# A graph network on one core: sums before one-hot products in each step of the build

## The reference

```python
# layer 0: gated, weighted sum over the edges
h = sigmoid(x @ W_gate + b_gate) * (x @ W)
out = segment_sum(edge_weight[:, None] * h[dst], src, N)
# layer 1: plain sum, then a matrix
out = segment_sum(x[src], dst, N) @ W.T + b
# layer 2: messages of both ends, summed, then an update
msg = concat(x[src], x[dst]) @ W_msg + b_msg
out = concat(x, segment_sum(msg, dst, N)) @ W_upd + b_upd
# layer 3: hypergraph convolution (nodes -> hyperedges -> nodes), batch norm, relu
out = relu(gamma * (o - mean(o)) * rsqrt(var(o) + eps) + beta)
```

## Time and profile before

| what | value |
|---|---|
| median of 3 runs | 2465.7 us |
| the profiled execution | 2461.7 us, its span 2459.8 us |
| mean granted TensorE clock | 0.978 |
| TensorE busy | 2293.2 us, 93% of the span |
| VectorE, ScalarE busy | 1444.7 us and 1279.8 us |
| HBM read and written | 257.85 MB, 92.19 MB |

### The profile page before, as it was taken

How to read it: one execution, slowest core, us unless ns; L and a number is a source line. 1 busy time by engine, 2 the same in 40 slices (tenths; PEclk the granted TensorE clock), 3 DMA queues, 4 the chain that set the end, 5 groups by cost and what they waited for, 6 DMA issues and landing times.

```text
span 2459.8 us, 72172 instructions
## 1 busy us (share of the span) xinstructions
PE 2293.2 (93%) x28669; PEld 2025.0 (82%) x28669; DVE 1444.7 (59%) x3422; ACT 1279.8 (52%) x2875; POOL 57.0 (2%) x57
## 2 busy tenths in 40 slices
PE   3689999999999989999889998999998999998997
PEld 3469898998899889988768887888887888887886
DVE  8779999998899988989643233234333111222223
ACT  3689999999899989989342222222221000011112
POOL 3500000000000000000000000000000000000000
PEclk9799999999999999999989999999999999999998
DMA  7799999999999999999989999999998999999997
GB/s 188 182 213 195 201 212 207 209 210 200 189 208 208 196 203 195 205 197 205 226 202 291 290 290 290 248 261 257 258 261 214 291 290 290 264 252 241 269 268 188
DMA packets 1528563, 569.80 MB, mean 232 GB/s; under 512 B 869815, under 2 KB 1526971, under 8 KB 1528152
## 3 DMA queue, kind: packets, MB, share of 16 engines
q1 hardware_dynamic: 1524709, 559.04, 104.0%
q0 software_dynamic: 1200, 4.10, 0.6%
q10 hardware_dynamic: 2370, 2.71, 0.4%
HBM read 257.85 MB, written 92.19 MB: 142 GB/s over the span
## 4 chain that ended last, share of the span: by engine, by line
PE 63%; SPq 16%; ACT 9%; DMA 5%; issue 4%; DVE 3%; POOLq 1%; another core or an unknown queue 0%; POOL 0%; DVEq 0%; ACTq 0%
PE ps L804 35%; SPq L542 8%; SPq L489 5%; ACT stage L1348 4%; PE ps L732 4%; ACT stage L1329 3%; PE ps L733 3%; PE ps L734 3%; PE ps L701 3%; PE ps L702 3%; PE ps L703 3%; PE ps L709 3%; DMA wt<-stage 3%; SPq L486 2%; PE ps L725 1%
## 5 line engine op out<-in xcount | busy, mean ns | idle before, releaser
L1348 ACT CAST stage<-ps 128x784 f16<-128x784 f32 x784 | 657.4, 838 | 18.0 <-PE ps L734 10.5
L804 PE MATMUL ps<-Ha,a_tiles 128*128 128x258 f16 x4606 | 523.9, 273 | 7.2 <-DVE Ha L1124 7.2
L732 PE MATMUL ps<-hot_c,hot_r 128*128 128x98 f16 x3136 | 502.7, 210 | 13.5 <-DVE hot_c L1046 10.4
L804 PEld LDWEIGHTS ps<-Ha,a_tiles 128*128 128x128 f16 x4606 | 449.9, 98 | 73.5 <-DVE Ha L1124 7.6
L733 PE MATMUL ps<-hot_c,hot_r 128*128 128x98 f16 x3136 | 500.4, 210 | 0.0
L734 PE MATMUL ps<-hot_c,hot_r 128*128 128x98 f16 x3136 | 498.8, 209 | 0.0
L701 PE MATMUL ps<-g_in,wt 128*128 128x128 f16 x2401 | 426.9, 220 | 29.2 <-DMA wt<-stage 20.1
L1329 ACT CAST stage<-ps 128x392 f16<-128x392 f32 x784 | 405.1, 517 | 43.4 <-PE ps L709 40.8
L703 PE MATMUL ps<-g_in,wt 128*128 128x128 f16 x2401 | 426.9, 220 | 0.0
L702 PE MATMUL ps<-g_in,wt 128*128 128x128 f16 x2401 | 426.9, 220 | 0.0
L1046 DVE TENSOR_TENSOR hot_c<-hot_c,meta 128x1568 f16<-128x1568 f16 x392 | 379.2, 967 | 0.0
(11 more groups left out here) (199 smaller groups left out, 2338.6 us busy)
## 6 DMA issues: line engine op xcount, KB each, us to landing
a_tiles<-counts_by_source SPq DMA_DIRECT2D x147, 1600.0 KB, 13.2
counts_by_source<-stage SPq DMA_DIRECT2D x49, 1600.0 KB, 8.7
meta<-edge_groups SPq DMA_DIRECT2D x26, 128.0 KB, 2.4
wt<-stage SPq DMA_TRANSPOSE x198, 6.2
gated_parts<-G SPq DMA_DIRECT2D x7, 448.0 KB, 5.4
g_in<-gated_parts SPq DMA_DIRECT2D x98, 32.0 KB, 6.0
out_x<-X SPq DMA_DIRECT2D x12, 256.0 KB
edge_table<-tab ACTq DMA_DIRECT2D x1, 2040.0 KB, 10.6
```

What stands on the lines that cost most here:

```text
L732: mm(into(0), rows_, codes(0), start=v == 0, stop=True, skip_group_check=True)
L804: last = mm(ps[:, sum_bank(ph, j, c), 0:PARTS], a_slot(ph, c, i), moving[:, i], start=i == 0, stop=i == TILES - 1)
L1348: a.copy(stage[:, b, 0:2 * FULL].rearrange("p (k i) d -> p k i d", k=2)[:, :, 0:TILES, u * SET_COLS:(u + 1) * SET_COLS], of).then_inc(s("h ...
```

## The change

In each round of `build` on TensorE the group of sums is issued in front of the wait for the one-hot set and the two units, where it was issued behind them. Nothing else differs: the same instructions, the same groups in the same step, the same semaphores and counts. The other engines' programs are unchanged.

```diff
                     for h in range(TILE_HOTS):
-                        pe.wait_ge(s("hot_ready"), j * TILE_HOTS + (h + 1))
-                        half_windows(j, c % 2, c, 2 * h)
-                        half_windows(j, c % 2, c, 2 * h + 1)
                         if not isinstance(n, int) or n >= 0:
                             g = sum_at(c, h)
                             if g == 0:
                                 loaded(n, 0)
                                 loaded(n, 1)
                             sum_some(n, cp, g)
+                        pe.wait_ge(s("hot_ready"), j * TILE_HOTS + (h + 1))
+                        half_windows(j, c % 2, c, 2 * h)
+                        half_windows(j, c % 2, c, 2 * h + 1)
```

## The result

The changed kernel takes 2533.48 us (median, 4 runs, 2529.95 to 2539.24) against 2465.8 us for the kernel before: 1.0274 times as long, 95% interval 1.0252 to 1.0296. The profiled execution took 2534.69 us with a span of 2532.8 us, 73.0 us more than before.

What follows compares the result with a forecast made beforehand. TensorE was busy in 93% of the span, with VectorE, ScalarE and DMA also close to full in the build. 52 + 18 - 2 = +68 us on the profiled 2461.7, plus 4.0 for the median, gave 2533 us; range 2500 to 2560.

Steps and rivals of the forecast that it cites:

- (a): In odd steps of the build, TensorE's wait for transposed tiles loses cover: 2.5 us longer per pair of steps.
- (g): The DMA chain up to the transposes may shorten as DMA engines get some air: 0.1 us a pair, -2 us.
- (b): SP's DMA chain starts earlier, 0.2 us for even tiles, under 0.1 for odd: 2.5 us a pair becomes 2.4.
- (f): TensorE's clock in the build drops after 14 of the 21 new stalls, 1.3 us each: 18 us.
- (e): The loop's two back edges, before steps 25 and 37: +1 us each, bounds 0 and 2.5.
- (c): ScalarE's copy of the even step's last turned block ends 0.8 us behind its last unit; the new stall hides it.
- (d): Each group of sums in the build needs a later addition by VectorE: cost 0, bounded at 221 us.
- A: Rival: in the build the wait moves as said, but the clock holds: +50 us, 2516 us; 20%.
- B: Rival: every new stall in the build drops the clock, in part for longer: 2553 to 2573 us; 10%.
- C: Rival: time from odd tile's last unit to its use shrinks to 24.2 us, clock unaffected: +35, 2501 us; 7%.
- D: Rival: faster, with odd tiles' transposes in by the even step's last unit and SP starting earlier: 2456 us; 4%.
- E: Rival: the order of groups in the build is immaterial, as ScalarE makes up for every stall: 2466 us; 4%.

Runs made afterwards that it cites:

- e1: Against the kernel before, sums put first in even steps only, odd steps in the old order: 2467.73 us, ratio 1.0024.
- e2: Against the kernel before, sums put first in odd steps only, even steps in the old order: 2516.42 us, ratio 1.0233.
- e4: The changed kernel with 40 matmuls added in front of the wait for the transposed tiles: 2513.56 us, 1.021 of the kernel before.
- e11: The changed kernel, but the fourth transpose and ScalarE's turned blocks are waited for at group 8 instead of group 0: 2450.02 us, 0.9965 of the kernel before.
- e3: The changed kernel, but SP's queue issues the store of the counts last, behind the four transposes: 2478.17 us, 1.0076 of the kernel before.

## Why the prediction was right

The mechanism was right, and e1, e2, e4 and e11 show it: a wait with its own date lost 2.5 us of cover in each pair of steps, and the clock fell on top of it. The time was forecast at 2533, the terms less exactly than that. Point by point:

- (a) The wait and its place: right. From U15 of step 1 to U15 of step 48 the build takes 1123.4 us in place of 1048.4, 75.0 more. In the 21 pairs away from the back edges 2.5 us more stand behind the wait, 52 us.
- (g), (b) R fell by more than the 0.2 us a pair forecast: from 25.1 to 24.8 us on the mean, 0.3 us. Nearly all of it is (g): the last transpose lands 24.5 us behind U15, before 24.7. (b) gave next to nothing, as SP's queue starts with the odd tiles 1.65 us behind U15 (1.66 before) and with the even ones 1.70 (1.76 before), and its waits for line 703, forecast to go, stayed (15.8 us, before 18.0). The wait's part is 21 x 2.2 = 46 us.
- (f) The clock: undersized. 18 drops in place of 14, at 1.5 us in place of 1.3: 27 us, less some 2 that step 3 had lost before as well. The 1.3 counted on a part of each drop lying inside the stall, but in 11 of 18 it fell behind S0. e4 shows the term to be real. The Trainium skill ("TensorE: Matmul & The Clock Gate", section "HAM oscillation — how this bites in real kernels") describes a kernel that waits some 3 to 5 us in front of each block of matmuls and loses the clock at every block. The changed kernel, with gaps of 2.0 to 4.5 us, shows nearly that, 18 of 21; e2, idle for 1.2 to 4.0 us, shows 2 of 21, so here it depends on more than there being a wait in each round.
- (e) The two back edges: +1.4 us each, forecast 1.
- (c) turned_out: hidden by the wait as said. In e3, where that cover was gone, S0 starts 0.98 us behind U15, forecast 0.8.
- (d) The additions: 0, as said. No wait at line 701 in the changed kernel's build was ended by one. In e2, where S15 and S0 stand together, one was away from the back edges, for 0.9 us.

The sum 46 + 25 + 3 = 74 us meets the 75 of the build. Its start came 2.6 us earlier in this execution, and from U15 of step 48 to the end of the span pass 1272.9 us, before 1272.3: with that the span's 73.0 us are accounted for. The errors did not cancel: the wait with the edges was forecast at 50 us (52 - 2) and was 49, the clock at 18 and was 25, so the forecast of 68 us is 5 us short of the 73.0 between the two profiled executions. That it meets the median to 0.5 us is luck: it starts from a profiled execution 4.0 us under the median of the kernel before, and the changed kernel's lies 1.2 us above its own. From U15 of one odd step to the next pass 45.0 to 49.7 us from step 5 on, away from the edges, where 45.5 to 47.7 was forecast without the price of a drop.

Of the rivals, A (the clock holds) did not come true in the changed kernel, but it is close to what e2 and e4 measured, 2516 and 2514 us for 2516. B fell with the three gaps in which the clock held and the 1.5 us a drop, C with R at 24.8 us on the mean, and D and E with the result itself.

What stays open: why the clock dropped after 18 of the gaps of the changed kernel, from 2.3 us on, and in the odd-only kernel after only one of four of 3.0 to 3.3 us. The length of the gap does not tell them apart (the changed kernel lost the clock behind 2.3 us and kept it behind 3.2), and I ran nothing that does.

## What to carry to other kernels

A wait with a date of its own (a transfer that nothing before it can hurry) should be read as a date, measured from the event that starts the transfer, and compared with the work that stands in front of it; moving the wait forward by one block of work then costs that block once per round, on top of what the engine loses when it restarts at a lower clock. Ask what the first consumer behind such a wait really reads: here the wait covered all four transposes of a tile where the next eight groups read the first and the third, and splitting it gave more than any reordering tried here.

## What was not expected of the hardware

A DMA transpose that is issued behind a 1600 KB store on the same queue lands later. In the changed order, with the same transfers, the fourth transpose lands 19.8 us behind U15 on the mean with the store behind all four, 24.5 us with the store between the second and the third, and 25.2 us with it directly in front of the fourth. In that last place the issue of the fourth transpose holds the queue for 8.4 us in place of 2.7, while the third lands at 16.1 us in place of 21.6. With the store behind all four, S0 never waited for them away from the back edges, though its cover was as short as 21.7 us.
